# A decoder layer on one Trainium2 core: the cross norm's statistics moved behind the cross maxima, and the last batch's transposed self scores put behind its self scores

## The reference

```python
x = _layernorm(x + _L0_attn_ref(x, w_qkv, w_proj, q_norm_w, k_norm_w))
x = _layernorm(x + _L0_xattn_ref(x, ctx_1024, ctx_1024, mask, Wq, Wk, Wv, Wo))
x = _layernorm(x + _L0_ffn_ref(x, routing_token, ...))
```

## Time and profile before

| | before |
|---|---|
| runs | 978.58, 981.06, 974.46 us; median 978.58 us |
| profiled execution | 978.16 us, span 976.4 us |
| PE busy | 888.3 us (91%) |
| DVE busy | 725.3 us (74%) |
| POOL busy | 537.9 us (55%) |
| ACT busy | 496.8 us (51%) |

### The profile page before, as it was taken

How to read it: one execution, slowest core, us unless ns; L and a number is a source line. 1 busy time by engine, 2 the same in 40 slices (tenths; PEclk the granted TensorE clock), 3 DMA queues, 4 the chain that set the end, 5 groups by cost and what they waited for, 6 DMA issues and landing times. The chain is left out here.

```text
span 976.4 us, 21698 instructions
## 1 busy us (share of the span) xinstructions
PE 888.3 (91%) x7712; PEld 689.7 (71%) x7712; DVE 725.3 (74%) x1764; ACT 496.8 (51%) x1063; POOL 537.9 (55%) x1047
## 2 busy tenths in 40 slices
PE   3367897999999999999999999999999999999886
PEld 2335565787868787777878787877778686767576
DVE  7788687878788878879787888788887877663411
ACT  1132444646475655656464756556464746455332
POOL 7554465646564756656565647657565656162421
PEclk9669898999999999999999999999999999999888
DMA  3794383727476654818275666738283656613000
GB/s 110 120 173 68 52 110 50 106 33 109 51 100 78 98 78 65 111 37 110 34 119 59 100 78 80 97 54 107 44 109 42 95 72 88 77 31 49 14 11 21
DMA packets 79644, 74.22 MB, mean 76 GB/s; under 512 B 8593, under 2 KB 78897, under 8 KB 79537
## 3 DMA queue, kind: packets, MB, share of 16 engines
q1 hardware_dynamic: 75008, 68.11, 50.5%
q10 hardware_dynamic: 4528, 4.73, 1.9%
HBM read 17.49 MB, written 4.20 MB: 22 GB/s over the span
## 5 line engine op out<-in xcount | busy, mean ns | idle before, releaser
L768 ACT ACTIVATE pr<-bank 128x384 f32<-128x384 f32 x512 | 240.0, 500 | 188.1 <-PE bank L370 187.0
L946 DVE TENSOR_REDUCE mx<-bank 128x3 f32<-128x384 f32 x512 | 266.4, 552 | 89.7 <-PE bank L370 87.5
L1311 POOL TENSOR_SCALAR_AFFINE_SELECT pr<-pr 128x256 f32<-128x256 f32 x512 | 222.1, 448 | 132.3 <-ACT pr L768 130.1
L370 PE MATMUL bank<-w,g 128*128 128x256 f32 x576 | 170.8, 389 | 1.1 <-ACT g L780 1.1
L370 PE MATMUL bank<-cmaskb,idb 128*128 128x256 bf16 x512 | 143.3, 280 | 27.7 <-DMA stk2k<-nat1k 13.7
L780 ACT ACTIVATE g<-bank,b 128x256 f32<-128x256 f32 x144 | 67.8, 473 | 83.5 <-PE bank L370 83.2
L1335 POOL TENSOR_TENSOR xTlow<-xT,xThigh 128x512 fp32r<-128x512 f32 x16 | 20.8, 1301 | 149.8 <-ACT xThigh L702 149.8
L370 PEld LDWEIGHTS bank<-w,g 128*128 128x128 f32 x576 | 89.6, 190 | 5.2 <-ACT g L780 1.5
L370 PEld LDWEIGHTS bank<-cmaskb,idb 128*128 128x128 bf16 x512 | 50.1, 98 | 50.5 <-DVE mx L946 22.5
L370 PE MATMUL bank<-stk2k,stk2q 97*128 97x128 bf16 (+1 forms) x512 | 85.1, 253 | 0.0
L370 PE MATMUL bank<-stk1q,stk1k 100*128 100x256 bf16 (+1 forms) x512 | 80.1, 254 | 2.4 <-DMA stk1q<-mT 1.0
(11 more groups left out here) (166 smaller groups left out, 1832.5 us busy)
## 6 DMA issues: line engine op xcount, KB each, us to landing
stk1q<-nat1q SPq DMA_DIRECT2D x90, 128.0 KB, 4.5
stk1k<-nat1k SPq DMA_DIRECT2D x90, 128.0 KB, 5.4
stk2k<-nat2k SPq DMA_DIRECT2D x90, 128.0 KB, 4.6
stk2q<-nat2q SPq DMA_DIRECT2D x90, 128.0 KB, 5.7
xT<-in_xT SPq DMA_DIRECT2D x16, 256.0 KB, 5.9
ctxT<-in_ctxT SPq DMA_DIRECT2D x16, 256.0 KB, 6.0
x<-in_x SPq DMA_DIRECT2D x16, 256.0 KB, 5.7
out_x<-x SPq DMA_DIRECT2D x16, 256.0 KB, 2.2
```

The costliest lines, as they stand in the source:

```text
L370: return nc.tensor.matmul(out, lhsT, rhs, start=start, stop=stop, skip_group_check=check)
L768: nc.scalar.activation(pr[:, h % (2 * HG), :], ring_bank("T", a, b, h)[:, 0:3 * P], ACT.Exp, scale=HD ** -0.5)\
L946: V.tensor_reduce(mx3[:, h, :], scored[:, 0:3 * P].rearrange("p (k t) -> p k t", k=3), AX.X, ALU.max, negate=True).then_inc(s_mx[a], 1)
L1311: G.affine_select(out=slot, in_=slot, compare_op=ALU.is_ge, fill=0.0, base=0, pattern=[[0, 2], [1, P]], channel_multiplier=-1).then_inc(s_ ...
```

## The change

Three things move; no arithmetic is added or left out.

In the steady steps VectorE's statistics of the cross residual go from between the cross maxima to behind `max_parts` of the cross scores. With them the norm `x2`, the scaled `xn` and the low part `xnl` go one place further back each, GpSimd's roots go from before T1's masks to between them (before head 2 and head 5), and the transposes of `xn` from T1's head 12 to T2's head 0.

In step 15 TensorE's order becomes S1(15), T1(15), S2(14), T2(14), where it was S1, S2, T1, T2. All of `ffn_out(12)`, the transposed maxima and `v2(14)` stand between S1(15) and T1(15); `x1T` and `q2` of batch 15 come into T2(14). The queues of the other engines follow; on VectorE the split of k, the first `divide_pair` and, between the maxima, the self norm of batch 15 come in.

In steps 16 and 17 the fillers are placed anew: S2(15) takes `hidden(13)`, and `ffn_out(13)` stands behind S2(15) as a whole.

```diff
-        turns = [turn for i in range(B + 1) for turn in (("S", 1, i), ("S", 2, i - 1), ("T", 1, i), ("T", 2, i - 1))
+        turns = [turn for i in range(B + 1)
+                 for turn in ((("S", 1, i), ("T", 1, i), ("S", 2, i - 1), ("T", 2, i - 1)) if i == B - 1 else
+                              (("S", 1, i), ("S", 2, i - 1), ("T", 1, i), ("T", 2, i - 1)))
...
+            def last_self_step(s):
+                c, f, l = s - 1, s - 2, s - 3
+                others = {}
+                def add(at, fn, *args):
+                    others.setdefault(at, []).append(lambda: fn(*args))
...
+                phase(lambda h: scores(1, s, h), others)
+                others = {}
+                for j in range(FCH):
+                    add(0, ffn_out, l, 0, j)
+                add(0, transpose_max, 1, s)
+                add(0, v2, c)
+                for j in range(FCH):
+                    add(0, ffn_out, l, 1, j)
+                add(LAST_K2_AT, k2, s)
+                for gr in range(NG - 1):
+                    add(HG * gr + VALUES_AFTER, values, 1, s, gr)
+                phase(lambda h: scores_t(1, s, h), others)
+                others = {}
+                add(LAST_OUT1_AT[0], values, 1, s, NG - 1)
+                add(LAST_OUT1_AT[1], out_proj, 1, s)
+                add(H, transpose_max, 2, c)
+                add(H, transpose_xn, f)
+                phase(lambda h: scores(2, c, h), others)
+                others = {}
+                add(LAST_Q2_AT[0], transpose_x1, s)
+                add(LAST_Q2_AT[1], q2, s)
+                for gr in range(NG - 1):
+                    add(HG * gr + VALUES_AFTER, values, 2, c, gr)
+                phase(lambda h: scores_t(2, c, h), others)
+            def last_cross_step(c):
...
+                add(0, values, 2, f, NG - 1)
+                add(TAIL_AT[0], out_tokens, f)
+                add(TAIL_AT[1], out_dims, f)
+                add(TAIL_AT[2], out_proj, 2, f)
+                add(TAIL_AT[3], v2, c)
+                for j in range(FCH):
+                    add(TAIL_HIDDEN_AT[j], hidden, l, j)
+                phase(lambda h: scores(2, c, h), others)
...
+                if s == B - 1:
+                    return last_self_step(s)
+                if c == B - 1:
+                    return last_cross_step(c)
...
-                if live(f):
-                    add(XNT_AT, transpose_xn, f)
+                if live(f) and not live(s):
+                    add(0 if f == B - 1 else XNT_AT, transpose_xn, f)
...
+                if live(f) and live(s):
+                    add(XNT_AT, transpose_xn, f)
...
-                    if h == COPY_XN_AT and live(f):
+                    if h == 0 and live(f) and not live(s) and not B - 3 <= f < B - 1:
                         copy_xn(f)
+                if s == B - 1:
+                    copy_group(1, s, NG - 2)
+                    high_part(2, s, 1, 0)
+                    copy_group(1, s, NG - 1)
                 for h in range(H):
-                    if live(s):
+                    if s == B - 1 and h == LAST_COPY_AT[0]:
+                        copy_x1(s)
+                        high_part(2, s, 0, 1)
+                    if B - 1 <= s <= B and h == LAST_COPY_AT[1]:
+                        copy_xn(f)
+                    if s == B - 1 and h == LAST_COPY_AT[2]:
+                        mid_part(2, s, 0, 1)
+                    if live(f) and live(s) and s < B - 1 and h == COPY_XN_AT:
+                        copy_xn(f)
+                    if live(s) and s < B - 1:
...
+            def last_self_step(s):
+                c, f, l = s - 1, s - 2, s - 3
+                maxima(1, s, {NORM2_AT: lambda: normalise_cross_heads(f), SPLITQ_AT: lambda: take_rest(2, c, 0, 1),
+                              LOWQ_AT: lambda: low_part(2, c, 0, 1)})
+                max_parts(1, s)
+                dve.wait_ge(s_x1c, f + 1)
+                add_residual(2, f, PROJ_BANK[2], x1c)
+                max_t(1, s)
+                statistics(2, f)
+                layer_norm(2, f)
+                scale2(f)
+                dve.wait_ge(s_x2b, l + 1)
+                add_residual(3, l, FFN_BANK, x2b)
+                statistics(3, l)
+                take_rest(2, s, 1, 0)
+                split_rest(2, s, 1, 0)
+                divide_pair(s, 0)
+                def self_residual():
+                    dve.wait_ge(s_x0, 16 * (s + 1))
+                    add_residual(1, s, PROJ_BANK[1], x0)
+                    statistics(1, s)
+                maxima(2, c, {LAST_DVE_AT[0]: lambda: divide_pair(s, 1), LAST_DVE_AT[1]: self_residual,
+                              LAST_DVE_AT[2]: lambda: layer_norm(1, s)})
+                max_parts(2, c)
+                max_t(2, c)
+                take_rest(2, s, 0, 1)
+                low_xn(f)
+                low_part(2, s, 0, 1)
+            def last_cross_step(c):
+                f, l = c - 1, c - 2
+                def residual_cross():
+                    dve.wait_ge(s_x1c, f + 1)
+                    add_residual(2, f, PROJ_BANK[2], x1c)
+                    statistics(2, f)
+                maxima(2, c, {TAIL_DVE_AT[0]: lambda: normalise_cross_heads(f), TAIL_DVE_AT[1]: residual_cross})
+                max_parts(2, c)
+                layer_norm(2, f)
+                max_t(2, c)
+                scale2(f)
+                dve.wait_ge(s_x2b, l + 1)
+                add_residual(3, l, FFN_BANK, x2b)
+                statistics(3, l)
+                low_xn(f)
...
-                    maxima(2, c, {RESID2_AT: residual_cross, MAXT_AT: max_rows, STAT2_AT: statistics_cross})
+                    maxima(2, c, {RESID2_AT: residual_cross, MAXT_AT: max_rows})
                     max_parts(2, c)
                 else:
                     residual_cross()
                     max_rows()
-                    statistics_cross()
-                if live(f):
-                    layer_norm(2, f)
+                statistics_cross()
                 if live(c):
                     max_t(2, c)
                 if live(i + 1):
                     split(1, i + 1, 0, 0)
                 if live(f):
-                    scale2(f)
+                    layer_norm(2, f)
                 if live(i + 1):
                     split(1, i + 1, 1, 1)
+                if live(f):
+                    scale2(f)
                 if first(i):
                     scale_w1()
-                if live(f):
-                    low_xn(f)
                 if live(l):
                     dve.wait_ge(s_x2b, l + 1)
                     add_residual(3, l, FFN_BANK, x2b)
...
                 if live(s):
                     divide_pair(s, 0)
+                if live(f):
+                    low_xn(f)
+                if live(s):
                     take_rest(2, s, 1, 0)
...
-                if live(f):
+                roots = {}
+                if live(f) and s == B - 1:
                     inverse_deviation(2, f)
                     inverse_norm2(f)
+                elif live(f):
+                    roots[RSTD2_AT[0]] = lambda: inverse_deviation(2, f)
+                    roots[RSTD2_AT[1]] = lambda: inverse_norm2(f)
                 if live(s):
-                    mask_probs(1, s, {})
+                    mask_probs(1, s, roots)
+                else:
+                    for h in sorted(roots):
+                        roots[h]()
                 roots = {}
-                if live(l):
+                if s == B - 1:
+                    inverse_deviation(3, l)
+                    inverse_deviation(1, s)
+                elif live(l):
                     roots[RSTD3_AT] = lambda: inverse_deviation(3, l)
-                if live(s):
+                if live(s) and s < B - 1:
                     roots[RSTD1_AT] = lambda: inverse_deviation(1, s)
...
-MAX2_AT, XNT_AT = 5, 12
+MAX2_AT, XNT_AT = 5, 0
 FFN1_AT = (0, 1, 2, 3, 4, 6, 8, 9, 10)
 K2_AT, OUT1_AT, QK1_AT, V1_AT = 1, (3, 9), (3, 6), 13
-MIDQ_AT, COPY2_AT, COPY_XN_AT, COPY_V1_AT = 1, 4, 13, 15
+LAST_K2_AT, LAST_OUT1_AT, LAST_Q2_AT, LAST_XNT_AT = 4, (2, 8), (1, 3), 6
+TAIL_AT = (3, 6, 9, 13)
+TAIL_HIDDEN_AT = (2, 2, 4, 5, 7, 8, 10, 11, 12)
+TAIL_LAST_AT = (6, 6, 11, 13, 13, 14, 14, 16, 16)
+COPY2_LAST, LAST_COPY_AT, LAST_DVE_AT, TAIL_DVE_AT = 2, (2, 3, 5), (3, 9, 12), (5, 12)
+MIDQ_AT, COPY2_AT, COPY_XN_AT, COPY_V1_AT = 1, 4, 1, 15
 COPY1_AT, SQ_AT = (0, 3, 3), (5, 7)
 QN_AT, NORM2_AT, SPLITQ_AT, LOWQ_AT, RESID2_AT, MAXT_AT, STAT2_AT = (1, 2), 5, 6, 8, 1, 3, 6
-RSTD3_AT, RSTD1_AT = 3, 13
+RSTD2_AT, RSTD3_AT, RSTD1_AT = (2, 5), 3, 13
```

More of the change, by code:

```diff
@@ L624, in phase @@
                         heads(h)
+            def last_self_step(s):
[3 more added lines that the diff above has]
+                    others.setdefault(at, []).append(lambda: fn(*args))
+                add(X1T_AT, transpose_x1, c)
+                add(OUT2_AT[0], values, 2, f, NG - 1)
+                add(Q2_AT, q2, c)
+                add(OUT2_AT[1], out_tokens, f)
+                add(OUT2_AT[2], out_dims, f)
```

(35 more changed lines are left out.)

1 line of the change is left out of this document (added).

## The result

The changed kernel takes 1032.06 us (median of 4 runs, 1029.74 to 1033.16) against 979.55 us for the kernel before in the same comparison: a ratio of 1.0543, 95% interval 1.0499 to 1.0587. Slower was right; the size, +52.5 us against a forecast of +29, was not, and the time lies outside the range of 984 to 1020. By the spans, 1029.6 against 976.4, the difference is 53.2 us.

A forecast was written before the change was run, and what follows sets the result against it. TensorE was taken to bound the steady steps. 978.16 us plus 16 (1.25 a step times 13 steady steps) plus 13 for the end gave 1007 us, with 992 to 1024 from the bounds and a stated range of 984 to 1020.

The forecast's parts named there:

- What bounds it: Steady steps: TensorE bounds, busy 59.20 of 60 us at full clock, so any new wait there is lost in full.
- The first group of values: Steady T1: later statistics delay roots and masks, so TensorE waits 0.55 us before the first values (0.5 to 0.7).
- The second group and xn: Steady T1: 0.35 us wait at the second values (0.1 to 1.0); 0.35 for xn's transposes (0 to 0.45).
- the S2 maxima give nothing back: Steady S2: the maxima lose their interruption, but S2 doesn't wait for them, so the gain is nothing.
- The end: Step 15 onward: the new order makes T2(15) start 13 us later, bounds 6 to 18.
- T2(14) has 12.0: the busy time of before: End: T2(14) priced at 12.0 us from its earlier busy time with work swapped in and out, bounds 10.0 to 14.2.
- Masks that keep up: Rival, steady T1: GpSimd's lead hides the later statistics, only the end costs; 991 us, chance 0.13.
- an even end: Rival, end: the new order breaks even, only the steady cost is left; 994 us, chance 0.12.
- nothing: Rival, whole kernel: waits land where TensorE waited anyway; 978 us, chance 0.06.
- faster: Rival, S2 and end: statistics no longer hold a bank (up to 11.7 us), 4.2 at the end; 962 us, chance 0.07.
- The third rival: Worse: long steady masks cost 6.5 us more, or half clock in T2(14) 5 more; put at 1013 us, chance 0.12.
- The second rival: End breaks even, if the last batch's self attention, done 11 us earlier, saves TensorE's lacks; 994 us, chance 0.12.

The follow-up runs named there:

- the two parts run alone: The change's steady part only, with the old end: 1013.90 us; its new end only, with the old steady steps: 998.61 us; kernel before 975.8 us.
- the roots early: Kernel before, with only GpSimd's cross-norm roots moved ahead of its low parts of x and the context: 973.36 us, ratio 0.9977.

## Why the prediction was wrong

**What bounds it** held. In the changed kernel, from 730 to 790 us, TensorE is busy 55.48 of 60 us at a clock of 1.00: the waits are lost in full.

**The first group of values** is the step that failed: "PE stands 704.65 - 704.10 = 0.55", measured 1.58. The chain was the right one (parts, statistics, `mv2`, root, two masks), and its middle links were right (statistics 0.96 against 1.01, root to first mask 0.97, 673.93 to 674.90). What was wrong is that I took the parts at what they cost with no mask beside them, and the masks at the mean of seven without the long one. The two casts take 0.38 more in sum, the two masks 0.67 more (0.62 + 0.85 against 0.80), which is the missing 1.0. Of this the run without q's low part shows 0.45 by taking the operation away. The rest, 0.6, no run took away: it is read from rows that stand beside each other, though without exception. In all eleven traces each cast of the parts that runs beside a mask takes 0.27 us or more, and each that doesn't at most 0.21. I had the row that told it, the mask of 0.85, and a rule beside it; I used both only for the second group, and as a rival of 0.12. They belonged in the sum: the change itself puts masks beside the parts and the split.

**The second group and xn** held: 0.33 against 0.35, and 0.47 against 0.35. That the S2 maxima give nothing back held as well; TensorE's heads there are 0.71 apart as before. In all, 2.4 a regular step instead of 1.25, and above my bound of 2.15. With the long steps, S1(15) ends 34.9 us later (884.27 against 849.33), not 16.

**The end** held as far as the first values of T1(15). Then two things were missing: TensorE's clock, and the waits inside T2(14). Times of the changed kernel, less these 34.9:

| | predicted | measured |
|---|---|---|
| T1(15) starts | 859.9 | 859.6 |
| first mask | 863.3 | 863.3 |
| first values | 864.9 | 864.9 |
| VectorE's split of k | 871.8 | 872.7 |
| T2(14) starts | 892.5 | 896.2 |
| S2(15)'s first scores | 904.5 | 912.5 |
| T2(15) starts | 929.4 | 937.7 |

Of the 8.3 us by which the end is late, 0.9 fall up to the split, behind a wait of 2.09 us at T1(15)'s first values and a second group that takes 1.51 instead of 0.86. Another 2.8 fall between the split and T2(14), where the slow `out_proj` holds VectorE's maxima (its wait of 3.39), and 4.3 in T2(14), which took 16.3 instead of 12.0 and lay above my upper bound of 14.2. The experiment with extra matmuls gives 5.1 of all this back, 2.0 of it in T2(14). The rest of T2(14) is not the clock. "T2(14) has 12.0: the busy time of before" is a second step that failed: at full clock T2(14) still took 14.2, as long as before, with TensorE busy 9.73. Taking work out of a phase that waits for other engines did not shorten it. In all T2(15) starts 21.1 us later against the steady end, not 13, and above my bound of 18.

I had named the clock too, as a rival with "a slow T2(14) takes 5 us more", and given it as an alternative to the long masks. Both happened, and neither was an alternative: the masks are long in the steady steps, and the clock falls behind the waits that I forecast for S2(14).

After T2(15) the changed kernel takes 56.9 us and the kernel before 59.8, where I had forecast no difference. This can't be put down to the change: five other runs with the old end took 56.5 to 57.6.

**The rivals.** Masks that keep up, an even end, nothing, and faster are all refuted by the two parts run alone. The third rival named both mechanisms, and priced the masks low (6.5 us, where casts and masks together cost 13 x 1.0 = 13) and the clock right (5 against 5.1), though less than half of it falls in T2(14). The second rival had a wrong premise: by the forecast's own chain T1(15) starts at 859.9, only 1.1 us and not 11 earlier than in the kernel before (861.0), since `ffn_out(12)` goes ahead of it.

## What to carry to other kernels

A wait that a change adds has a second price: the work behind it can run at half clock, so forecast it in the sum wherever the engine idles for microseconds, not as a mishap beside it. Price a phase that waits for other engines by its length, not by the busy time in it. When a change shifts an engine's work in time, price it at what it takes beside its new neighbours; a single long row in the old trace, like the mask of 0.85, tells which pairs hold each other up. And where a queue has small roots ahead of a row of masks, look for an earlier gap to put them in before looking behind.

## What the runs showed that I had not expected

Even a 128x32 cast on VectorE took 0.34 to 0.39 us instead of 0.18 when masks ran on GpSimd beside it: both casts of the cross parts in 12 steps of the changed kernel, and in one step of the kernel before. With the roots early they took 0.44 and 0.32 beside the norm's output and masks, and that kernel was the faster one all the same: what a long instruction costs depends on what waits for it. And a single wait of 1.58 us in a steady step that is otherwise full was in some steps followed by a granted clock of 0.79 over 8 us, which cost about 1.2 us; with the wait at 1.13 us, or with xn's transposes back in T1, no step from 275 us on was longer than the rest.
